# Sorted expert tiles whose weights are streamed from DRAM into four fixed buffers, in place of seven resident experts picked by a register

## What is computed

```python
logits = x @ w_router                                  # 8 experts, the last one is empty
probs = softmax(logits); topk_vals, topk_idx = top_k(probs, 2)
up = einsum('btd,edh->ebth', x, w_up)                  # 7 experts, 128 -> 512
gate = silu(einsum('btd,edh->ebth', x, w_gate))
exp_out = einsum('ebth,ehd->ebtd', up * gate, w_down)  # 512 -> 128
# for the best expert only:
out = 2.0 * topk_vals[..., 0:1] * (exp_out of the expert topk_idx[..., 0], or 0 for the eighth)
shared = x @ ws_up * silu(x @ ws_gate) @ ws_down
x = x + gb * (out + shared)
```

## Time and profile before

| what | value |
|---|---|
| median of 3 runs | 1013.0 us (1011.45 to 1015.21) |
| profiled execution, its own time | 1013.29 us |
| its span in the profile | 1011.6 us |
| mean granted clock of PE | 0.963 |
| busy share PE, PEld, DVE, ACT, POOL | 86%, 59%, 77%, 74%, 62% |

### The profile page before, as it was taken

One profiled execution on the slowest core, in us unless ns is written; L12 is line 12 of the kernel. 1 busy time (PEld: TensorE's weight loads), 2 busy tenths in 40 slices (PEclk: granted clock), 3 DMA queues, 4 the chain that ended last, 5 costly groups with the idle time before them and its releaser, 6 DMA issues.

```text
span 1011.6 us, 18872 instructions
## 1 busy us (share of the span) xinstructions
PE 871.0 (86%) x5652; PEld 600.7 (59%) x5652; DVE 774.0 (77%) x1842; ACT 746.4 (74%) x2019; POOL 622.3 (62%) x876
## 2 busy tenths in 40 slices
PE   4337989989998999899989998998999999968893
PEld 3335656657666666666656666666666665635662
DVE  5989969967996799679867987798787676745543
ACT  6426897788879878888887888788888788534442
POOL 3156767867785778678857885787666562260232
PEclk9759999999999999999999999999999999998997
DMA  9000000000010010010000000000000004112003
GB/s 226 3 0 8 1 23 23 22 23 23 23 28 18 27 31 23 12 34 23 23 23 24 22 23 23 23 23 23 9 2 2 2 3 188 64 43 59 17 25 102
DMA packets 45602, 32.66 MB, mean 32 GB/s; under 512 B 8032, under 2 KB 43488, under 8 KB 45504
## 3 DMA queue, kind: packets, MB, share of 16 engines
q1 hardware_dynamic: 44288, 28.95, 9.8%
q0 software_dynamic: 1216, 2.51, 0.7%
HBM read 18.30 MB, written 12.36 MB: 30 GB/s over the span
## 4 chain that ended last, share of the span: by engine, by line
PE 61%; DVE 24%; ACT 7%; issue 4%; another core or an unknown queue 1%; POOL 1%; DMA 1%; ACTq 0%; DVEq 0%; POOLq 0%; SPq 0%
PE psum L1194 21%; PE psum L1219 7%; PE psum L1208 6%; PE psum L1302 5%; PE psum L1135 5%; PE psum L1179 4%; DVE pcs L848 4%; PE psum L1199 3%; DVE arena L796 3%; ACT probs L564 3%; DVE accs L904 3%; PE psum L1244 2%; DVE psum L893 2%; PE psum L1181 2%; PE psum L1196 2%
## 5 line engine op out<-in xcount | busy, mean ns | idle before, releaser
L1194 PE MATMUL psum<-QK 128*128 128x128 f32 (+3 forms) x1024 | 371.7, 448 | 4.6 <-ACT QK L543 4.6
L564 ACT ACTIVATE probs<-psum,negmax 128x128 f32<-128x128 f32 (+3 forms) x512 | 266.8, 529 | 106.3 <-DVE negmax L893 75.5
L391 POOL TENSOR_TENSOR R<-pcs 128x512 f32<-128x512 f32 x128 | 207.2, 1639 | 63.9 <-DVE pcs L848 46.5
L893 DVE CUSTOM_DVE_ANT_0 psum<-psum,causal 128x384 f32<-128x384 f32 (+1 forms) x256 | 156.8, 636 | 74.7 <-PE psum L1199 74.7
L1194 PEld LDWEIGHTS psum<-QK 128*128 128x128 f32 x1024 | 163.8, 192 | 48.9 <-issue 41.2
L417 POOL TENSOR_TENSOR coef<-rden,wslot 128x2 f32<-128x2 f32 x256 | 67.8, 265 | 175.1 <-DVE rden L899 175.0
L848 DVE TENSOR_TENSOR pcs<-psum,arena 128x512 f32<-128x512 f32 x256 | 161.6, 672 | 0.0
L904 DVE SCALAR_TENSOR_TENSOR accs<-probs,coef,accs 128x128 f32<-128x128 f32 (+3 forms) x256 | 157.4, 615 | 1.0 <-ACT accs L573 1.0
L573 ACT ACTIVATE accs<-probs,coef 128x128 f32<-128x128 f32 (+3 forms) x256 | 148.6, 580 | 11.7 <-POOL coef L417 10.8
L1208 PE MATMUL psum<-ident,accs 128*128 128x128 f32 x640 | 116.2, 280 | 46.1 <-ACT QK L543 41.6
L543 ACT ACTIVATE QK<-psum 128x384 f32<-128x384 f32 x256 | 126.4, 494 | 0.8 <-PE psum L1181 0.7
(11 more groups left out here) (217 smaller groups left out, 1466.0 us busy)
## 6 DMA issues: line engine op xcount, KB each, us to landing
weight_halves<-whl SPq DMA_DIRECT2D x48, 128.0 KB, 2.2
arena<-weight_halves SPq DMA_DIRECT2D x7, 768.0 KB, 7.4
wst<-in_L_ffn_w_up_dram SPq DMA_DIRECT2D x14, 128.0 KB, 2.5
wst<-in_L_ffn_w_gate_dram SPq DMA_DIRECT2D x14, 128.0 KB, 2.5
wst<-in_L_ffn_w_down_dram SPq DMA_DIRECT2D x14, 128.0 KB, 2.4
sorted_rows<-arena SPq DMA_DIRECT2D x1, 1430.0 KB, 11.0
QK<-sorted_rows SPq DMA_DIRECT2D x5, 260.0 KB, 4.3
x<-in_L_attn_x_dram SPq DMA_DIRECT2D x4, 256.0 KB, 4.1
```

What stands on the lines that cost most here:

```text
L391: pool.tensor_tensor(R[u][:, :, :, 0:3:2, half * HALF:(half + 1) * HALF].rearrange("p t e j f -> p (t e) j f"), halves(pc, half), halves(p ...
L564: act.activation((expB if e else expA)[:, k % (4 if e else 3), 0:w], area, ACT.Exp, scale=1.0 if k % TB < 2 else -1.0, bias=negmax[k % 4][ ...
L893: dve.tensor_tensor_reduce(score_area(k, e), score_area(k, e), causal[:, T - w:T], -1.0, 3e38, ALU.add, ALU.min, accum_out=negmax[k % 4][: ...
L1194: pe.matmul(o, QK[:, u, e, rows], QK[:, u, 2, 0:w], start=True, stop=False)
```

## The change

The sorted tiles no longer pick their expert out of seven resident ones. `w_tile` has four places. For each tile in turn SP reads the expert's number into a register and loads that expert's three matrices from `weight_halves` into place j % 4, with a semaphore for each place (`wt0` to `wt3`). The first four loads follow `ids_done`; the load of tile j from 4 on is issued when the down product of tile j-4 is done, behind the reads of the sorted rows. On PE the weights are the stationary operand for gate and up (24 matmuls of 128 columns), as for the shared expert, so that the hidden values come out with hidden units on partitions: `flip_hidden`, its semaphore and its PSUM round trip are gone, and PE uses no register. Gate and up have a semaphore each (`gu_mm`, `up_mm`), so that SiLU may begin when the gate half is done; this holds for the shared steps too. The semaphores of the angle steps and of the router's weights are merged into counters.

```diff
-        w_ex = arena[:, 0:(E - 1) * 1536]...
+        AHEAD = 4
+        w_tile = arena[:, 0:AHEAD * 1536].bitcast(F16).rearrange("p (r l k n) -> p r l k n", l=2, k=3, n=HID)
...
             sp.wait_ge(S["prod_done"], 4 * NH)
-            for e in range(E - 1):
-                if e == 5:
-                    sp.wait_ge(S["pv_done"], NH // 2)
-                sp.dma_start(w_ex[:, e, :, :, :], halves_d[e + 1]).then_inc(S["ex_in"], 16)
+            sp.wait_ge(S["ids_done"], 1)
+            def tile_weights(j):
+                e = sp.value_load(ids_u[0:1, j:j + 1], min_val=0, max_val=E - 2)
+                sp.dma_start(w_tile[:, j % AHEAD, :, :, :],
+                             halves_d[1:E, :, :, :, :][bass.ds(e, 1)].rearrange("a p l k n -> p (a l) k n")
+                             ).then_inc(S[f"wt{j % AHEAD}"], 16)
+            for j in range(AHEAD):
+                tile_weights(j)
             sp.wait_ge(S["sent"], 16 * NT)
             for g in range((SORTED + 3) // 4):
...
+            for j in range(AHEAD, SORTED):
+                sp.wait_ge(S["down_mm"], 16 + j - AHEAD + 1)
+                tile_weights(j)
...
             def hidden_row(i):
                 dve.wait_ge(S["silu_done"], i + 1)
-                if 2 <= i < 18:
+                dve.wait_ge(S["up_mm"], i + 1)
+                if i >= 2:
                     dve.wait_ge(S["hid_lo"], i - 1)
-                elif i >= 18:
-                    dve.wait_ge(S["hf_mm"], i - 17)
...
-            def expert_gate_up(j, e):
-                i = 16 + j
+            def expert_gate_up(j):
+                i, r = 16 + j, j % AHEAD
                 pe.wait_ge(S["xt_lo"], j // 4 + 1)
+                pe.wait_ge(S[f"wt{r}"], 16 * (j // AHEAD + 1))
                 free_gates(i)
                 rows = [xsT[:, l, j * P:(j + 1) * P] for l in range(2)]
-                for dst, k in ((bank[i % 2], 1), (bank[2 + i % 2], 0)):
-                    mm_ = three(dst[:, :], rows, [half_of(e, l, k, 0, HID) for l in range(2)], True, True)
-                mm_.then_inc(S["gu_mm"], 1)
-            def flip_hidden(j):
-                ...
+                for dst, k, done in ((bank[i % 2], 1, "gu_mm"), (bank[2 + i % 2], 0, "up_mm")):
+                    for c_ in range(TB):
+                        mm_ = three(dst[:, c_ * P:(c_ + 1) * P],
+                                    [w_tile[:, r, l, k, c_ * P:(c_ + 1) * P] for l in range(2)], rows, True, True)
+                    mm_.then_inc(S[done], 1)
...
             for j in range(SORTED):
-                of_tile.append(pe.value_load(ids_u[0:1, j:j + 1], min_val=0, max_val=E - 2))
-                expert_gate_up(j, of_tile[j])
+                expert_gate_up(j)
...
-                if j >= 1:
-                    flip_hidden(j - 1)
                 if j >= 2:
-                    expert_down(j - 2, of_tile[j - 2])
-            flip_hidden(SORTED - 1)
+                    expert_down(j - 2)
```

More of the change, by code:

```diff
@@ L633, in upper_half @@
                     act.wait_ge(S["down_mm"], i - 1)
[L634 to L637, removed]
+                act.activation(hid16[i % 2][:, 0, :], hidden[i % 2], ACT.Copy).then_inc(S["hid_hi"], 1)
             def sorted_high(g):
@@ L676, in _ @@
                     upper_half(15 + j)
[L677 to L680, removed]
+                if j >= 2:
+                    expert_row(j - 2)
+            expert_row(SORTED - 1)
         @block.vector
@@ L959, in low_hidden @@
                 dve.wait_ge(S["hid_hi"], i + 1)
-                flipped = hidden[i % 2] if i < 16 else bank[4 + i % 2][:, :]
-                dve.tensor_tensor(hid16[i % 2][:, 1, :], flipped, hid16[i % 2][:, 0, :], ALU.subtract
+                dve.tensor_tensor(hid16[i % 2][:, 1, :], hidden[i % 2], hid16[i % 2][:, 0, :], ALU.subtract
                                   ).then_inc(S["hid_lo"], 1)
@@ L1002, in weights @@
                 dve.wait_ge(S["r_exp"], 1)
[L1003 to L1006, removed]
+                dve.tensor_reduce(rm[:, 2, :], rr[:, 0, :, :], AX_X, ALU.add).then_inc(S["r_norm"], 1)
+                dve.wait_ge(S["r_norm"], 1)
+                dve.reciprocal(rm[:, 3, :], rm[:, 2, :]).then_inc(S["r_norm"], 1)
+                dve.wait_ge(S["r_norm"], 2)
                 dve.wait_ge(S["wo_mm"], 2 * B)
@@ L1317, in shared_gate_up @@
                 rhs = [h2[:, l, t_ * T:(t_ + 1) * T] for l in range(2)]
-                for dst, k in ((bank[i % 2], 1), (bank[2 + i % 2], 0)):
-                    mm_ = three(dst[:, :], [w_sh[:, l, k, c_ * P:(c_ + 1) * P] for l in range(2)], rhs, True, True)
-                mm_.then_inc(S["gu_mm"], 1)
+                for dst, k, done in ((bank[i % 2], 1, "gu_mm"), (bank[2 + i % 2], 0, "up_mm")):
+                    three(dst[:, :], [w_sh[:, l, k, c_ * P:(c_ + 1) * P] for l in range(2)], rhs, True, True
+                          ).then_inc(S[done], 1)
             def shared_down(i):
@@ L1349, in sorted_columns, with expert_down @@
                 mm_.then_inc(S["xt_mm"], 1)
[L1351 to L1355 removed]
+            def expert_gate_up(j):
+                i, r = 16 + j, j % AHEAD
                 pe.wait_ge(S["xt_lo"], j // 4 + 1)
+                pe.wait_ge(S[f"wt{r}"], 16 * (j // AHEAD + 1))
                 free_gates(i)
                 rows = [xsT[:, l, j * P:(j + 1) * P] for l in range(2)]
[L1359 to L1375 removed]
+                for dst, k, done in ((bank[i % 2], 1, "gu_mm"), (bank[2 + i % 2], 0, "up_mm")):
+                    for c_ in range(TB):
+                        mm_ = three(dst[:, c_ * P:(c_ + 1) * P],
+                                    [w_tile[:, r, l, k, c_ * P:(c_ + 1) * P] for l in range(2)], rows, True, True)
+                    mm_.then_inc(S[done], 1)
+            def expert_down(j):
                 i = 16 + j
@@ L1384, in expert_down @@
                                 [hid16[i % 2][:, l, c_ * P:(c_ + 1) * P] for l in range(2)],
-                                [half_of(e, l, 2, c_ * P, (c_ + 1) * P) for l in range(2)], c_ == 0, c_ == TB - 1)
+                                [w_tile[:, j % AHEAD, l, 2, c_ * P:(c_ + 1) * P] for l in range(2)],
+                                c_ == 0, c_ == TB - 1)
                 mm_.then_inc(S["down_mm"], 1)
@@ L1421, in _ @@
                     token_rows(3)
-            pe.wait_ge(S["ex_in"], 16 * (E - 1))
-            pe.wait_ge(S["ids_done"], 1)
-            of_tile = []
             shared_down(14)
```

38 lines of the change are left out of this document (16 added, 22 removed).

## The result

The changed kernel took 1033.38 us in the median of 4 runs (1028.8 to 1036.54), the kernel before 1012.23 us beside it (4 runs). The ratio is 1.0182, with a 95% interval of 1.0148 to 1.0217: 1.8% slower, at 1032 us forecast. The profiled execution took 1035.12 us with a span of 1033.3 us, 21.7 us more than the span of before.

What follows compares the result with a forecast made beforehand. Weight-load latency behind one round of lead was to bound the sorted loop: 1003.0 + 5.3 + 13.7 = 1022.0 us, plus 8.5 for the clock gives a 1030.5 span, with 1.7 more 1032 us. Range 1018 to 1047.

Steps and rivals of the forecast that it cites:

- The lead: Sorted-tile weight loads: the four-place ring leaves one round (gate/up j-1 and down j-3, 2.01 us) of lead.
- L: Sorted loop: time from the end of a down product to the gate/up it allows, 5.2 us, bounds 4.8 and 6.5.
- The pair: Sorted loop: two tiles close together, then a gap of some 2.6 us; 2.01 + 5.2 = 7.2 us per two tiles.
- Two loads in flight: Sorted-tile loads: two at most, 2.0 to 2.6 us apart, 4.3 us each; slowing each other would prove it wrong.
- The clock: Sorted loop: some gaps end at the lower clock, 1.0 us for each of 8.5 pairs, 8.5 us.
- The tail: From the last gate/up to the end: 19.0 us, of which 5.3 to the last scatter's issue and 13.7 as before.
- A: Sorted loop, the forecast itself: load latency sets the pace, clock partly lost; range 1024 to 1041 us; 52%.
- B: Sorted loop: load latency sets the pace but the clock stays; 1024 us, or 1020 with a 4.8 us latency; 17%.
- C: Sorted loop: every pair at the lower clock, 17 us; 1041 us, or 1050 with latency near 6.0 as well; 17%.
- D: Sorted loop: loads are hidden and every round is 2.01 us from tile 5 on; time 995 us; 6%.
- E: Gate/up of sorted tiles: PE's weight loads set the matmul spacing, 24 take 2.35 us; time 1041 us; 3%.
- F: Stall during the scatters, 12 us by estimate, changes: gone 1020 us (3%), doubled 1044 us (2%).

Runs made afterwards that it cites:

- e8: Changed kernel with each tile's load cut in two, gate/up matrices loaded after gate/up of j-4, down matrix after down of j-4: 1002.5 us, ratio 0.9862.
- e4: Changed kernel with SP loading experts in a fixed order, without a register: loop 71.2 us, time 1011.7 us beside 1004.4 for the kernel before.
- e9: Changed kernel loading only the upper halves of the matrices (384 KB) from tile 4 on: loop 71.5 us, time 1028.4 us.
- e11: Changed kernel, four places, with 20 idle matmuls before each gate/up from tile 4 on: loop 75.6 us, time 1030.0 us.
- e6: Changed kernel run and profiled again unchanged, on a second chip: loop 77.6 us, 1030.7 us against 1017.6 for the kernel before.
- e2: Changed kernel with eight ring places instead of four: loop 45.5 us, time 985.6 us, ratio 0.984 to the kernel before.
- e7: Changed kernel's stationary weights without flips, but seven experts kept resident and picked by PE's register: loop 82.8 us, 1038.0 us, ratio 1.0191.

## Why the prediction held, point by point

The mechanism held: the load's latency behind a lead of one round. That the sum came out within 2 us of the measured time is in part luck, as the clock was priced some 6 us too high, while the slower pairs, the late loads and a start that came 5.3 us late were not in the sum.

- **The lead.** Four buffers give a lead of one round: shown, by rings of 3, 5, 6 and 8 places and by e8.
- **L.** 5.2 us were put down and 5.2 measured: 0.75 on SP (0.1 + 0.6 + 0.2 forecast) and 4.43 from issue to use (4.3 forecast). e4 and e9 confirm the parts.
- **The pair.** 7.2 us forecast, 7.43 measured. The 2.17 us from the start of gate/up to the end of the last down matmul, its drain included, belongs there and not 2.01. That is 1.4 us over the loop. The pairs themselves dissolved after tile 7, with waits of 1.1 to 1.9 us before every gate/up and not before every second.
- **Two loads in flight.** The forecast took 4.3 us for each and named a slowing of one by the other as a sign that it is wrong. Tile 7's load took 5.75 us. It was issued close behind tile 6's: round 4, at the lower clock, had run into the time of round 5, so that their down products, which free the two places, ended 2.0 us apart. From tile 8 on the loads started 3.3 us or more apart and took 4.3 to 4.7 us, but for one of 5.10 (tile 11).
- **The whole loop.** Without the clock the forecast has gate/up 21 at 1003.0 - 930.4 = 72.6 us behind gate/up 0; 78.06 were measured. The odd tiles show where the 5.5 us lie. Gate/up 5 came 16.20 us after gate/up 0 in place of 15.0 (0.8 by the slow round of tile 4, 0.4 by a later down product), eight pairs at 7.4 us in place of 7.2 give 1.6, the loads of tiles 7 and 11 give 1.5 and 0.6, the slow round of tile 7 gives 0.6.
- **The start.** Gate/up 4 came 12.60 us after gate/up 0; 942.85 - 930.4 = 12.45 was forecast.
- **The clock.** This is the term that was mis-sized: 1.0 us for each of 8.5 pairs, 8.5 us, where e11 shows 2.0 to 2.5 (1.4 directly on the odd tiles above, the rest through the load of tile 7 as far as the rows tell). The forecast expected a wait of 2.6 us in every pair and a dip behind half of them; such waits came only before tiles 4 and 6. At 3.7 us a tile, with waits under 2 us, the clock stayed at 1.00. The Trainium skill's loop in which every tile starts cold ("TensorE: Matmul & The Clock Gate", "HAM oscillation — how this bites in real kernels") is the ring of three, with waits of 5.2 us, and not the changed kernel.
- **The tail.** 19.0 us forecast, 19.4 measured, 21.0 before. The gain has a source that neither the section on the change nor the forecast names: ACT now scales the down product of tile j-2 in its round j (`expert_row`), where it scaled that of j-3. No run parts it from the rest.
- **Attention and the shared stage.** Nothing was forecast; the profiled execution was 5.3 us late there, which other executions of either kernel are by 0 to 5.5 us. In the sum this made good what the clock was priced too high: 10.4 + 8.5 = 18.9 us of loss forecast, and 17.85 + 5.3 + 0.1 - 1.6 = 21.7 measured in the two spans. The loop itself was forecast at 81.1 us and took 78.06. The nearness of 1032 to 1033.4 is luck to that extent; beside e6, one run on another chip, the loss was 13.1 us (1030.7 against 1017.6).
- **The rivals.** Of the clock's cost A had 8.5 us, B nothing and C 17: the 2.0 to 2.5 of the runs lie nearer to B, while the loop as a whole, with its slower pairs and late loads, came out nearer to A. D needs more places than four, and is then real. E is refuted by e2. F's stall moved, but with the chip and not with the change.

## What to carry to other kernels

Count a ring's lead in rounds from the instruction that frees a place to the one that needs its new content, not in places: four places gave one round here, and a load has to fit its latency, its bytes and the issuer's register work inside that lead. Free each part of a place by the instruction that last reads it (e8), or add places while memory lasts (e2, the fastest, 1.6% under the kernel before). And try the two halves of a change apart: here the wide matmuls on resident weights, and the narrow ones on streamed weights with lead enough, were both good designs, and the mixture of e7 was worse than either (1.9% over the kernel before).

## What the runs showed of the hardware that was not expected

- With PE waiting 5.2 us between rounds the granted clock stayed low for a whole loop (0.60, ring of three); with waits of 1.1 to 1.9 us it stayed at 1.00, though PE was busy 28.2 of 48.9 us only. In e9 it stayed at 1.00 for 38 us with waits of 1.5 and 0.5 us in turn, and was 0.77 over the next 22 us, in which single waits were 3.34 and 2.94 us long.
- Seven resident matrices with register addresses cost PE's queue some 24 operations a tile, and 24 matmuls then took 2.27 us in place of 1.50, about 0.05 us for each address.
- A 768 KB load takes 4.4 us to its use alone, 5.75 and 6.06 us when issued 2.2 us behind another (tile 7 in the two profiles of the changed kernel), and 7.1 us to landing in the median with several in flight at 375 GB/s, at no loss when the lead covers it.
- The stall of some 12 us during the scatters was there in every profile but those of one chip, in kernels that share that code. Its cause stays open, and with it the 8 to 13 us by which the kernel before differs between chips (1004.4, 1012.2 and 1017.6).
